# A graph layer with residual and layer norm: when the first loads of the second part are issued

## The reference

```python
row, col = src, dst
h_self = x @ W_lin + b_lin
messages = x[col] @ W_msg + b_msg
msg_sum = segment_sum(messages, row, n_nodes)
counts = segment_sum(ones, row, n_nodes)
h_agg = msg_sum / maximum(counts, 1.0)[:, None]
h = relu(concatenate([h_self, h_agg], axis=1) @ W_upd + b_upd)
out = layernorm(x + h)
```

## Time and profile before

| | |
|---|---|
| median of 3 runs | 1325.19 us |
| span of the profiled execution | 1375.4 us |
| PE busy | 1203.5 us, 88% of the span |
| DVE busy | 997.9 us, 73% |
| ACT busy | 710.7 us, 52% |
| POOL busy | 498.1 us, 36% |
| DMA | 156.27 MB, mean 114 GB/s |

### The profile page before, as it was taken

One profiled execution on the slowest core, in us unless ns is written; L12 is line 12 of the kernel. 1 busy time (PEld: TensorE's weight loads), 2 busy tenths in 40 slices (PEclk: granted clock), 3 DMA queues, 4 the chain that ended last, 5 costly groups with the idle time before them and its releaser, 6 DMA issues. The chain is left out here.

```text
span 1375.4 us, 41041 instructions
## 1 busy us (share of the span) xinstructions
PE 1203.5 (88%) x15996; PEld 715.2 (52%) x15996; DVE 997.9 (73%) x2543; ACT 710.7 (52%) x1027; POOL 498.1 (36%) x503
## 2 busy tenths in 40 slices
PE   1949899887884799999999999999999999999996
PEld 1948798876871344444444444444444444444443
DVE  7999999999995266666666666666666666666665
ACT  0313333310111476666666766666666666666664
POOL 3000000000004555555455555555555555555540
PEclk9979999998876799999999999999999999999998
DMA  7213233213407244444444444444444344444420
GB/s 103 97 47 102 97 111 106 77 45 104 111 5 231 66 123 129 124 137 137 135 137 139 135 138 138 137 137 137 122 125 117 120 120 132 136 137 138 138 62 12
DMA packets 120430, 156.27 MB, mean 114 GB/s; under 512 B 32314, under 2 KB 90279, under 8 KB 120166
## 3 DMA queue, kind: packets, MB, share of 16 engines
q1 hardware_dynamic: 95932, 105.62, 24.3%
q0 software_dynamic: 23024, 47.31, 13.8%
q10 hardware_dynamic: 1290, 0.74, 0.2%
HBM read 130.46 MB, written 23.17 MB: 112 GB/s over the span
## 5 line engine op out<-in xcount | busy, mean ns | idle before, releaser
L610 ACT ACTIVATE big<-slot 128x768 bf16<-128x768 f32 x800 | 608.2, 809 | 332.2 <-PE slot L1326 305.7
L1326 PE MATMUL slot<-big 128*128 128x384 bf16 x2600 | 498.4, 328 | 45.0 <-ACT big L610 38.2
L675 POOL DMA_INDIRECT big<-x,dst_at x400 | 407.0, 1018 | 335.8 <-PE slot L1326 153.6
L989 DVE TENSOR_SCALAR big<-big,iota_k 128x512 bf16<-128x512 f16 x650 | 220.5, 371 | 332.9 <-PE slot L1326 305.0
L1326 PEld LDWEIGHTS slot<-big 128*128 128x128 bf16 x2600 | 216.0, 97 | 305.8 <-issue 126.8
L1340 PE MATMUL acc<-big 32*128 32x385 bf16 x6400 | 335.7, 325 | 9.4 <-issue 9.3
L1340 PEld LDWEIGHTS acc<-big 32*128 32x128 bf16 x6400 | 133.4, 93 | 184.7 <-issue 123.6
L999 DVE TENSOR_TENSOR big<-col_lo,iota_lo 128x512 bf16<-128x512 f16 x400 | 166.3, 416 | 0.0
L669 POOL MEMSET big<- 128x4 bf16 x6 | 0.3, 96 | 412.4 <-issue 412.4
L1240 PE MATMUL acc<-big 125*100 125x64 f16 x1600 | 85.3, 215 | 25.8 <-DVE big L877 25.7
L679 POOL DMA_INDIRECT big<-x,sp_i x75 | 76.9, 1026 | 84.6 <-PE acc L1363 40.1
(11 more groups left out here) (150 smaller groups left out, 810.9 us busy)
## 6 DMA issues: line engine op xcount, KB each, us to landing
big<-rows SPq DMA_DIRECT2D x25, 2048.0 KB
big<-in_x SPq DMA_DIRECT2D x48, 256.0 KB, 3.3
x<-big SPq DMA_DIRECT2D x24, 384.0 KB, 2.6
big<-x,dst_at POOLq DMA_INDIRECT x400
base<-big SPq DMA_DIRECT2D x24, 256.0 KB, 2.5
big<-x SPq DMA_DIRECT2D x32, 192.0 KB, 2.4
big<-base SPq DMA_DIRECT2D x24, 256.0 KB
out<-big SPq DMA_DIRECT2D x24, 256.0 KB
```

Source lines behind the costliest of these rows:

```text
L610: act.activation(xg[n % NX][:, :, 0:F3], slot[n % 2][:, :, 0:F3], ACT.Copy).then_inc(s["xg_ready"], 1)
L675: pool.indirect_dma_start(out=xg_d[:, c, 0:F3], out_offset=None, in_=x3_dram, in_offset=bass.IndirectOffsetOnAxis(ap=dst_at[:, q, c:c + 1] ...
L989: last = nc.vector.tensor_scalar(W[R_ % NW_][:, k, :].rearrange("p (c h n) -> p c h n", c=4, h=4), brow[q % NB].rearrange("p (h c n) -> p ...
L1326: ins = nc.tensor.matmul(slot[n % 2][:, j, 0:F3], W[R_ % NW_][:, k, (c % 4) * P:(c % 4 + 1) * P], xwin[:, win_at(c) + k, :], start=k == 0, ...
```

## The change

On SP, load_brow(1) is taken from its place behind the tail windows, ahead of the flag. It now stands in `fast()` ahead of load_x4(0) and waits until `W_ready` is at 4 (RUNS // 4). Behind it, load_x4(0) waits until `W_ready` is at 8 (RUNS // 2). All later loads stand behind these two waits. In `general()` DVE no longer waits for the second buffer, which is not loaded on that path now.

```diff
             load_brow(0)
             with sp.Fori(0, CP - 60) as c:
                 load_window(bass.ds(c + 60, 1), xwin[:, bass.ds(c * 3 + NWIN_A, 3), :], 3, s["tail_wins_loaded"])
-            load_brow(1)
 
             sp.wait_ge(s["flag_known"], 1)
...
+                sp.wait_ge(s["W_ready"], RUNS // 4)
+                load_brow(1)
+                sp.wait_ge(s["W_ready"], RUNS // 2)
                 load_x4(0)
                 for q in range(Q):
                     if q + 1 < Q:
...
             def general():
                 made[0] = before_branch
-                for k in range(NB):
+                for k in range(1):
                     dve.wait_ge(brow_loaded[k], 16)
```

## The result

The changed kernel takes 1327.35 us (median of 20 runs) against 1325.08 us before (20 runs); the ratio is 1.0023, 95% interval 1.0014 to 1.0032. That is 3.0 us slower (1.9 to 4.2), a little over the 0.2% that this kernel's measurement can tell. The ratio is taken over all the runs of both kernels; the two medians alone lie 2.3 us apart. The forecast was no change, 1325.0 us; the time is inside the stated range, but the kind of outcome is not the one forecast.

What follows compares the result with a forecast made beforehand. It took the kernel as bound by PE over 25 steady quads. Every part of the change was put at 0, with the stall outside the timed runs or unmoved, giving 1325.0 us; range 1300 to 1328 us.

Steps and rivals of the forecast that it cites:

- The stall: PE's completions held from 434.92 to 458.64 us in the profile; priced, with the slow clock behind, at 24.0 us.
- Rival A: The load burst at the second part's start causes a real stall; moving loads removes it: 1301.2 us, chance 0.28.
- The gap of 50.2 us: Profiled span 1375.4 us against timed median 1325.19 us: at least that much of the trace is not in the forecast time.
- The step that split 50.2 us between the stall and the quads: Over 25 quads alone, 2.0 us each; if the stall is part of it, 26.2 us remain, 1.0 us a quad.
- Items 1 to 3: Delayed brow(1), delayed x loads, and SP's queue behind the two waits: readers have spare time, cost 0 each.
- Item 2: The x loads wait for the eighth one-hots; readers in quad 1 leave 30 us spare, cost 0.
- Item 5: DMA relieved from 423 to 431 us, brow(1) beside gathers until 438: taken as 0, bounds -1.1 and +5.6 us.
- Rival B: In quad 0 brow(1) lies on gathers PE needs: at most 5.6 us slower, 1330.8 us, chance 0.11.

Runs made afterwards that it cites:

- the second profile: The kernel before, profiled once more with no edit: ratio 1.0008 [0.9996, 1.0019], span 1321.4 us, quad 0 44.36 us.
- run 4: Not an experiment: a stretch of PE's gather, aggregate and pair matmuls in quad 0; PE's landing wait at its pair was 1.2 us in the changed kernel.
- run 7: Not an experiment: a later such stretch of PE in quad 0, whose pair needs chunk 7; PE waited 1.24 us before, 3.21 us in the changed kernel.

## Why the prediction was wrong, point by point

**The stall.** Right, and the most of the working's worth: the excess was priced at 24.0 us of the profiled execution and taken out of the timed runs. From flag to quad 1 the first profile of before took 491.07 - 423.33 = 67.7 us, the second 44.36: 23.4 us. PE's rows of the first profile:

```profile
423.33 0.58 PE L1305 MATMUL slot<-flag_c,ones 128*128 128x1 f32 x2 [6.56 <-DVE flag_c L964]
...
491.07 1.51 PE L1326 MATMUL slot<-big 128*128 128x384 bf16 x8 [0.67 <-ACT big L610]
```

Rival A (0.28) fell with that. The reason I gave for the stall, records of the burst's DMA packets, is not shown: the second profile has a burst of 3019 packets between 424 and 437 us against 3395, and no stall. Rival A's path, an instruction fetch behind the loads, was read from "exactly one packet" of the instruction queue. There are two in that stretch, one on each of two queues, and the second profile has the same two and no stall:

```profile
q8 instruction: 1, 0.02, 0.5%
q14 instruction: 1, 0.01, 0.2%
```

What caused the stall stays open. The gap of 50.2 us set one execution against others; in the second profile the span is 2.0 us under the time of the same execution. The step that split 50.2 us between the stall and the quads held too: 36.3 - 35.2 = 1.1 us a quad was the rest.

**Items 1 to 3.** The places, the waits and the slack of the readers were right: brow(1) went at 431.06 us and the loads of x at 435.07, and no reader waited for either, in any of the experiments. But "cost 0" was worked out from the readers of the moved loads alone. Item 2 did not ask what the loads of x would run beside once they go at 435 us; that is POOL's series of gathers. With only these loads moved the profile's quad 0 is 2.2 us longer, though the timed runs do not tell that loss from nothing.

**Item 5 is the step that failed.** It put the effect of brow(1) on POOL's gathers at 0, from the bounds -1.1 to +5.6 us. The runs show 3.0 us in its place: in the profiles PE waits 4.3 to 4.4 us for gathers in quad 0 where it waited 1.2 us before, and runs 1.6 us longer at a lower clock behind the second wait. The 0 had two reasons, both wrong.
- "I see no wait of PE for a landing before." That was read from an execution in which one run of PE took 23 us, just where PE would have waited. A stall gives every producer that is not stalled time to catch up, so no slack can be read in it or behind it. The second profile shows a wait of 1.24 us and one of the weight load of 0.53 us.
- "The gathers met as full a queue before and were in time." Before, the queue was full only until PE came to its first pair; then the DMA share falls. Windows of the second profile of before from 430 to 442 us, and below of the changed kernel:

```profile
430.00:436.00 6.00, 5.86 (x78) 2.62 (x76) 4.64 (x14) 3.58 (x6) 4.48 (x6) 1.00 0.90 229
436.00:442.00 6.00, 6.00 (x86) 2.81 (x84) 3.19 (x10) 4.20 (x6) 4.48 (x6) 1.00 0.40 69
```

```profile
436.00:442.00 6.00, 4.79 (x60) 2.13 (x59) 2.09 (x6) 3.03 (x4) 4.60 (x5) 1.00 1.04 342
442.00:448.00 6.00, 3.30 (x49) 1.36 (x46) 2.07 (x6) 3.03 (x4) 4.48 (x6) 1.00 1.00 204
```

The burst used to lie on the first gathers, from 424 to 434 us, when PE was in its first runs (the granted clock is 0.68 from 424 to 430 us) and needed one spill; the change put it on the later ones, which have little or none.

**Rival B was the answer, at 0.11.** Mechanism (brow(1) on top of the gathers), place (the pair of run 4) and sign were right; the measured 3.0 us is about half of its 5.6 us. It lacked the second place, run 7, where the rare gathers stand in front of chunk 7 and over half of the wait arises. It also lacked the clock: behind the wait of 3.21 us the granted clock of the changed kernel is 0.64 from 449 to 453 us (windows above), that is partly at the 1.2 GHz level. Quad 0 is 5.1 us longer than in the second profile of before, and 4.8 of these are accounted for: the waits grew by 3.2 us, the clock cost 1.6 us. The timed runs show 3.0 us. The executions compared are not typical ones: that of before took 1323.39 us, 1.8 us under its median, and that of the changed kernel 1330.31 us, 3.0 us over its own. How often the clock falls in the runs that were only timed is not shown.

**The chances.** Given the profile at hand, 0.11 for B was too low by my own working: the text put a gather at 7 us from issue to use and its landing at 437.4 to 438.7 us against a need at 438, which is an even chance, and then set it aside.

## What to carry to other kernels

A load that is moved away from a burst is moved onto something: price it against what its queue neighbours deliver in the new place and how much slack these have there, not only against its own reader. Of the places tried for brow(1) the best was the old one, ahead of the flag, where the other transfers had most slack. A wait of PE can cost more than its length: here the 1.6 us at a lower clock came on top. If a profile's span is far from the median of the timed runs, take a second one before anything is read from the first: the waits that matter may be hidden under one that happens once.

## What the runs showed of the hardware that I had not expected

- In one profiled execution of twelve, PE started the 26 matmuls that were left of one run over 23 us, and ACT and DVE, which waited for that run, went on within 0.12 us of each other (457.68 us, and 457.80 in the earlier trace rows). No timed run is long enough to hold it. The quads behind it took 36.3 us in place of 35.2, with a second wait of PE for ACT in each:

```profile
564.17 1.51 PE L1326 MATMUL slot<-big 128*128 128x384 bf16 x8 [0.66 <-ACT big L610]
574.22 1.51 PE L1326 MATMUL slot<-big 128*128 128x384 bf16 x8 [0.90 <-ACT big L610]
```

  So the same code ran in two steady rhythms, 3% apart, and kept the slower one to the end of this execution. That the disturbance put it there, and what held it, is not shown.
- An indirect gather of 128 rows of 768 bytes took 3.7 us from issue to use beside other gathers alone (chunk 7 in the second profile of before), 4.4 us with only the loads of x moved to set 8, 5.15 us with only brow(1) beside it, and 7.3 and 6.7 us beside all the loads of the changed kernel. It was issued as early as before: 18.4 us behind PE's matmul for the flag in the changed kernel and 18.5 before. So the landing is what came late, not POOL's issue.
- PE's granted clock fell in or behind waits of 1.95, 2.37, 3.02, 3.13 and 3.21 us at run 7. It stayed at 1.00 behind waits of 0.48 and 1.24 us there, and behind one of 2.18 us at run 4. So the wait's length alone does not decide it; what does was not tried.
